# Half-row query stacks for two cross-attention groups, and one group's row sums taken earlier, in a two-attention transformer layer

## What is computed

```python
xn1 = _ln(x, g1, be1)
sa = _mha(xn1, xn1, Wq_s, bq_s, Wk_s, bk_s, Wv_s, bv_s, causal=True)
x = x + (sa @ W1 + b1)
xn2 = _ln(x, g2, be2)
ca = _mha(xn2, encoder_out, Wq_c, bq_c, Wk_c, bk_c, Wv_c, bv_c, causal=False)
x = x + (ca @ W2 + b2)
xn3 = _ln(x, g3, be3)
ff = jax.nn.relu(xn3 @ Wf1 + bf1) @ Wf2 + bf2
return x + ff
```

## Time and profile before

| | |
|---|---|
| median of three runs | 587.0 us |
| profiled execution, its time | 590.07 us |
| its span, first to last instruction | 588.2 us |
| mean granted clock of TensorE | 0.927 |
| PE busy | 490.6 us (83%) |
| DVE, ACT, POOL busy | 333.1, 316.0, 189.6 us |
| DMA moved | 48.11 MB, mean 82 GB/s |

### The profile page before, as it was taken

How to read it: one execution, slowest core, us unless ns; L and a number is a source line. 1 busy time by engine, 2 the same in 40 slices (tenths; PEclk the granted TensorE clock), 3 DMA queues, 4 the chain that set the end, 5 groups by cost and what they waited for, 6 DMA issues and landing times.

```text
span 588.2 us, 8820 instructions
## 1 busy us (share of the span) xinstructions
PE 490.6 (83%) x3296; PEld 284.2 (48%) x3296; DVE 333.1 (57%) x645; ACT 316.0 (54%) x622; POOL 189.6 (32%) x291
## 2 busy tenths in 40 slices
PE   1588974999999999989988888685379897999887
PEld 1375651443434343444433234341235176888877
DVE  3155885878788787867864044253455275363340
ACT  3674420757676767645576767355043972445360
POOL 2498870131212121221213424215611193030200
PEclk9989998899999999989999999788558788999999
DMA  8145846016162525250112774215941520101001
GB/s 284 58 134 177 203 139 119 0 26 105 35 109 60 94 45 106 56 90 2 34 34 79 162 148 79 57 33 156 176 95 23 145 60 0 37 1 37 19 18 37
DMA packets 31082, 48.11 MB, mean 82 GB/s; under 512 B 8832, under 2 KB 25728, under 8 KB 28928
## 3 DMA queue, kind: packets, MB, share of 16 engines
q1 hardware_dynamic: 30972, 47.54, 35.1%
q10 hardware_dynamic: 68, 0.02, 0.0%
HBM read 30.66 MB, written 12.03 MB: 73 GB/s over the span
## 4 chain that ended last, share of the span: by engine, by line
PE 59%; DVE 13%; ACT 9%; DMA 9%; issue 3%; POOL 2%; SPq 2%; ACTq 0%; DVEq 0%
PE ps L1197 12%; PE ps L1058 11%; PE ps L1167 9%; PE ps L1114 9%; PE ps L1278 6%; DVE max_a L1355 5%; PE ps L1136 4%; ACT arena_p L926 4%; DMA stacks<-shift_t 3%; PE ps L1044 3%; DMA stacks<-qc_parts 2%; PE ps L1153 2%; DVE hid_r L1458 2%; PE ps L1118 2%; DVE max_b L1355 2%
## 5 line engine op out<-in xcount | busy, mean ns | idle before, releaser
L926 ACT ACTIVATE arena_p<-ps 128x512 f32<-128x512 f32 (+4 forms) x416 | 191.4, 543 | 150.8 <-PE ps L1167 149.8
L1355 DVE TENSOR_REDUCE max_a<-ps 128x1 f32<-128x512 f32 (+4 forms) x280 | 158.9, 619 | 73.9 <-PE ps L1114 61.8
L1114 PE MATMUL ps<-stacks 96*128 96x77 bf16 (+4 forms) x640 | 139.0, 293 | 31.1 <-DMA stacks<-qc_parts 18.2
L1167 PE MATMUL ps<-stacks 99*128 99x512 bf16 (+1 forms) x448 | 142.6, 352 | 16.6 <-ACT arena_p L926 7.7
L1114 PEld LDWEIGHTS ps<-stacks 96*128 96x128 bf16 x640 | 55.5, 106 | 97.1 <-DVE max_a L1355 38.2
L1197 PE MATMUL ps<-arena_p,v_group 128*32 128x512 f32 (+3 forms) x896 | 95.9, 541 | 0.3 <-POOL arena_p L790 0.3
L790 POOL TENSOR_SCALAR_AFFINE_SELECT arena_p<-arena_p 128x512 f32<-128x512 f32 x64 | 39.9, 635 | 161.4 <-ACT arena_p L926 161.4
L1167 PEld LDWEIGHTS ps<-stacks 99*128 99x128 bf16 x448 | 42.3, 100 | 80.5 <-ACT arena_p L926 37.1
L1355 DVE TENSOR_REDUCE max_b<-ps 128x1 f32<-128x384 f32 (+3 forms) x88 | 52.9, 635 | 22.6 <-PE ps L1118 22.3
L1058 PE MATMUL ps<-wf2r,hid_r 128*128 128x256 f32 x384 | 47.2, 284 | 4.9 <-DVE hid_r L1458 3.8
L732 POOL TENSOR_TENSOR xs<-xs,row 128x256 f32<-128x256 f32 x48 | 39.6, 856 | 33.3 <-DVE xn L1312 33.3
(11 more groups left out here) (79 smaller groups left out, 501.3 us busy)
## 6 DMA issues: line engine op xcount, KB each, us to landing
arena_h<-out_t SPq DMA_DIRECT2D x16, 256.0 KB, 4.3
recips<-recip_rows SPq DMA_DIRECT2D x8, 512.0 KB
q_parts<-parts SPq DMA_DIRECT2D x8, 384.0 KB, 2.6
k_parts<-parts SPq DMA_DIRECT2D x8, 384.0 KB, 2.7
qc_parts<-parts SPq DMA_DIRECT2D x8, 384.0 KB, 3.0
stacks<-qc_parts SPq DMA_DIRECT2D x8, 384.0 KB, 6.4
stacks<-q_parts SPq DMA_DIRECT2D x7, 384.0 KB, 5.2
stacks<-k_parts SPq DMA_DIRECT2D x7, 384.0 KB, 7.6
```

The source lines that it names most:

```text
L926: nc.scalar.activation(probs[0:a.kp, a.probs_slot(g, ui), h, k * BANK:k * BANK + width], ps[0:a.kp, unit % S_BANKS, 0:width], ACT.Exp, sca ...
L1114: ins = nc.tensor.matmul(m_bank(use)[:, o:o + w], q_stack[0:ROWS, slot, h, t * P:(t + 1) * P], k_self[0:ROWS, slot, h, s0:s0 + w] if a.cau ...
L1167: ins = nc.tensor.matmul(ps[:, unit % S_BANKS, lo - k * BANK:hi - k * BANK], k_rows(a, ROWS_S, g, h, i * P), q_stack[:, a.slots[g % a.nb], ...
L1355: nc.vector.tensor_reduce(dst, m_bank(use)[:, 0:nh * w].rearrange("p (h w) -> p h w", h=nh), AX.X, ALU.max).then_inc(use_read, 1)
```

## The change

The query parts of groups 4 and 5 go to a DRAM tensor of their own, `qh_dram`, in which the 512 rows of a chunk lie together. Their stacks are loaded by halves: three DMAs of 192, 128 and 64 KB for chunk 2's rows, as soon as chunk 2's store for this pair has landed, and three more for chunk 3's. In the list the loads become: group 4 first half 27.5, group 5 first half 28.5, group 4 second half 31.5, group 5 second half 31.55, group 6 whole at 31.6 (was 40.0). The stack in SBUF is laid out half by half; chunks 4 to 7 of a group wait for its second half, chunks 0 to 3 for the first only.

For cross group 1 the copy of the second half of the product moves from 19.24 to 16.5, its packing from 20.15 to 16.6, its reciprocal, store and spread from 23.4 to 17.5, 17.6 and 17.7; its division stays behind chunk 3's last split. The packing of group 2 moves from 27.15 to 31.58, between the half loads and the load of group 6, and the packing of group 3 (33.75) now stands behind the load of group 6. The spread of group 3 moves from 56.0 to 53.4, ahead of the load of group 7.

```diff
+HALVED = (4, 5)
-            add(nxt + (0.46 + 0.5 * n) * CROSS_US, "copy", CROSS, g, n)
+            add(END + 16.5 if (g, n) == (1, 1) else nxt + (0.46 + 0.5 * n) * CROSS_US, "copy", CROSS, g, n)
         if g < NG - 2:
-            add(nxt + 1.1 * CROSS_US, "packed", CROSS, g)
-        if g == 1:
-            add(nxt + 1.6 * CROSS_US, "inverted", CROSS, g)
-            add(nxt + 1.62 * CROSS_US, "stored", CROSS, g)
-            add(nxt + 1.64 * CROSS_US, "spread", CROSS, g)
-            add(nxt + 2.9 * CROSS_US, "divided", CROSS, g)
+            add(END + (16.6, 31.58)[g - 1] if g in (1, 2) else nxt + 1.1 * CROSS_US, "packed", CROSS, g)
+    add(END + 17.5, "inverted", CROSS, 1)
+    add(END + 17.6, "stored", CROSS, 1)
+    add(END + 17.7, "spread", CROSS, 1)
+    add(END + 31.9, "divided", CROSS, 1)
-    add(END + 56.0, "spread", CROSS, 3)
+    add(END + 53.4, "spread", CROSS, 3)
-    for g, t in zip(range(NG // B, NG), (31.5, 31.6, 40.0, 53.5)):
-        add(END + t, "load", CROSS, g)
+    for g, half, t in ((4, 0, 27.5), (5, 0, 28.5), (4, 1, 31.5), (5, 1, 31.55), (6, None, 31.6), (7, None, 53.5)):
+        add(END + t, "load", CROSS, g, half)
...
+    qh_dram = nc.dram_tensor("qc_half_parts", (PARTS, 2, 2, GW, CHUNK), BF16).ap()
+        q_cross = q_stack.rearrange("p n h t -> p n (h t)").rearrange("p n (s h t) -> p n s h t", s=2, h=GH)
+                if 4 * (n // 2) + 2 * hh == HALVED[0]:
+                    a = qh_dram[:, n % 2, :, :, :]
+                    return CHUNK, BQ_C + hh, [(a.rearrange("p g r t -> (g r) p t"), 0, CHUNK)]
...
+            def load_half_stack(g, half, arrived, blk, part, n, same):
+                rows_of = qh_dram[part:part + (1 if same else n), half, g - HALVED[0], :, :]
+                rows_of = rows_of.rearrange("p (d h) t -> d p (h t)", d=D)
+                to = q_cross[blk * D:(blk + n) * D, CROSS.slots[g % CROSS.nb], half, :, :].rearrange("p h t -> p (h t)")
+                sp.dma_start(to, rows_of.to_broadcast([D, n, GH * CHUNK]) if same else rows_of).then_inc(arrived, 16)
...
+                        g, half = what
+                        for n in range(2) if half is None else [half]:
+                            u = U_QC + 2 * (2 * (g // (NG // B)) + n) + g % (NG // B) // 2
+                            sp.wait_ge(parts_out[u % 4], parts_landed(u))
+                        load_stacks(a, g, range(len(Q_RUNS)), half)
...
+                    if not a.causal and g in HALVED:
+                        pe.wait_ge(q_half[g % 2], 16 * len(Q_RUNS))
+                    else:
+                        pe.wait_ge(s.q_in[g % a.nb], 16 * n_loads)
+                elif not a.causal and g in HALVED and t == CT:
+                    pe.wait_ge(s.q_in[g % a.nb], 16 * len(Q_RUNS) * (g // a.nb + 1))
```

More of the change, by code:

```diff
@@ L259, in order @@
     for g, t in enumerate([7.1 * SELF_US, 7.15 * SELF_US, 7.2 * SELF_US, END + 0.5]):
-        add(t, "load", CROSS, g)
-    for g, t in zip(range(NG // B, NG), (31.5, 31.6, 40.0, 53.5)):
-        add(END + t, "load", CROSS, g)
+        add(t, "load", CROSS, g, None)
+    for g, half, t in ((4, 0, 27.5), (5, 0, 28.5), (4, 1, 31.5), (5, 1, 31.55), (6, None, 31.6), (7, None, 53.5)):
+        add(END + t, "load", CROSS, g, half)
     w2 = END + 70.0
@@ L430, in build @@
         half_in = sem("half_in")
+        q_half = [sem(f"q_half{p}") for p in range(2)]
         parts_out = [sem(f"parts_out{s}") for s in range(4)]
@@ L570, in load_run, with load_stacks @@
                              rows_of.to_broadcast([D, n, GH * T]) if same else rows_of).then_inc(arrived, 16)
-            def load_stacks(a, g, runs=range(2 * len(Q_RUNS))):
+            def load_half_stack(g, half, arrived, blk, part, n, same):
[3 more added lines that the diff above has]
+                sp.dma_start(to, rows_of.to_broadcast([D, n, GH * CHUNK]) if same else rows_of).then_inc(arrived, 16)
+            def load_stacks(a, g, runs=range(2 * len(Q_RUNS)), half=None):
                 s, slot = of[a], a.slots[g % a.nb]
@@ L583, in load_stacks @@
                 for n in runs:
-                    if n < len(Q_RUNS):
+                    if half is not None:
+                        load_half_stack(g, half, s.q_in[g % a.nb] if half else q_half[g % 2], *Q_RUNS[n], True)
+                    elif n < len(Q_RUNS):
                         load_run(q_dram if a.causal else qc_dram, q_stack[0:ROWS, slot, :, :], g, s.q_in[g % a.nb],
@@ L772, in split_shift @@
                 pool.wait_ge(maxima, n + 1)
-                m = max_a[:, g % 2, :, :].rearrange("p h i -> p (h i)")
+                m, to = max_a[:, g % 2, :, :].rearrange("p h i -> p (h i)"), neg_m[:, :]
+                if not a.causal and g in HALVED:
+                    m = max_a[:, g % 2, :, :].rearrange("p h (s i) -> p s h i", s=2)
+                    to = to.rearrange("p (s h i) -> p s h i", s=2, h=GH)
                 base = 5 * n
-                pool.tensor_scalar(neg_m[:, :], m, -1.0, None, ALU.mult).then_inc(shift_step, 1)
+                pool.tensor_scalar(to, m, -1.0, None, ALU.mult).then_inc(shift_step, 1)
                 pool.wait_ge(shift_step, base + 1)
@@ L1095, in k_rows, with q_columns @@
                 return k_self[0:n, a.slots[g % a.nb], h, lo:lo + P] if a.causal else k_ctx_row[0:n, at:at + P]
+            def q_columns(a, g, n, h, lo, hi):
+                slot = a.slots[g % a.nb]
+                if a.causal or g not in HALVED:
+                    return q_stack[0:n, slot, h, lo:hi]
+                t0 = lo // CHUNK * CHUNK
+                return q_cross[0:n, slot, lo // CHUNK, h, lo - t0:hi - t0]
             def chunk(use, a, g, c):
@@ L1106, in chunk @@
                         n_loads += 2 * (len(QP) - len(Q_RUNS))
-                    pe.wait_ge(s.q_in[g % a.nb], 16 * n_loads)
+                    if not a.causal and g in HALVED:
+                        pe.wait_ge(q_half[g % 2], 16 * len(Q_RUNS))
+                    else:
+                        pe.wait_ge(s.q_in[g % a.nb], 16 * n_loads)
                     if g == 0 and not a.causal:
                         pe.wait_ge(s.k_in, 16 * len(KP))
+                elif not a.causal and g in HALVED and t == CT:
+                    pe.wait_ge(s.q_in[g % a.nb], 16 * len(Q_RUNS) * (g // a.nb + 1))
                 diagonal = a.causal and s0 + w == (t + 1) * P
@@ L1113, in chunk @@
                     o = (h - h0) * w
-                    ins = nc.tensor.matmul(m_bank(use)[:, o:o + w], q_stack[0:ROWS, slot, h, t * P:(t + 1) * P],
+                    ins = nc.tensor.matmul(m_bank(use)[:, o:o + w], q_columns(a, g, ROWS, h, t * P, (t + 1) * P),
                                            k_self[0:ROWS, slot, h, s0:s0 + w] if a.causal
@@ L1168, in score @@
                                                k_rows(a, ROWS_S, g, h, i * P),
-                                               q_stack[:, a.slots[g % a.nb], h, q0 + lo - off:q0 + hi - off],
+                                               q_columns(a, g, ROWS_S, h, q0 + lo - off,
+                                                         q0 + hi - off),
                                                start=True, stop=True)
```

## The result

The changed kernel takes 592.08 us (median of ten runs, 590.13 to 593.85); the kernel before, in ten runs on the same chip, 587.06 (585.53 to 590.26). The ratio is 1.0071, 95% interval 1.0053 to 1.009. It is slower by 0.71%, or 4.2 us of 587 (the two medians alone lie 5.0 us apart, inside the interval's 3.1 to 5.3), and so outside the 2.9 us that I had called no change.

A forecast was written before the change was run, and what follows sets the result against it. The DMA queue and SP's order were taken to bound 405 to 439 us. Score 0 of group 5 coming 2.3 us later, halved by the clock to +1.15 with group 1's 0.46 inside, gave +1.2: 588.2 us, range 584.4 to 591.8.

The forecast's parts named there:

- within 0.5%: Whole kernel: time within about 2.9 us of the kernel before, either way; chance 0.60.
- rival 2: Halves at 2.25 us or above, SP late, group 3's sums at 426.0, group 7's load put off 4.0: +4, 591.0; chance 0.22.
- The bound: From 405 to 439 us the DMA queue and SP's filling order limit the kernel, no engine's arithmetic.
- Group 1, +0.46: Group 1's reciprocal ahead of chunk 2's norm on DVE delays the block up to the stores by 0.46 us, bounds 0 and 0.55.
- The halves: Groups 4 to 6: data 4 us earlier, but group 3's sums at 424.4 keep group 4's shift issue at 425.9, as before.
- The spread: Group 3's spread ahead of group 7's load puts that load off 3.0 us, to 438.35; score 0 of group 5 +2.3.
- The clock: Clock back no later than before, at 445.4; leftover 2.3 us of PE work then runs at twice the speed: +1.15.
- To the end: Behind 445 us the order is the old one and everything shifts alike.
- The signs: Profile after: group 3's reciprocal at 424 to 425, PE waiting 3 to 4 us for group 7, landing near 438.
- the slower side: Whole kernel: slower by more than 2.9 us; chance 0.23.
- Rival 1: Faster: group 3's sums at 423.2, group 7's load put off only 2.0, clock maybe sooner: -1 to -3.5, 585.0; chance 0.20.
- Rival 3: From 405 to 439 us the halves gain nothing in the full queue; only the reciprocal's 0.46 is left: 587.5; chance 0.08.

The follow-up runs named there:

- after_spread_back: The changed kernel with group 3's spread put back behind group 7's load: 588.0 us, ratio 1.0002 to the kernel before.
- halves_pack3_first: The changed kernel with group 3's spread back behind group 7's load and group 3's packing ahead of group 6's load: 584.11 us, ratio 0.9954 to before.
- best: The changed kernel with group 3's packing ahead of group 6's load, its spread last, all spreads on 16 engines, group 1 at its old place: 578.3 us, ratio 0.9843.
- pack3_group1_back: halves_pack3_first with group 1's copy, packing, reciprocal, store and spread at their old places: 584.07 us, ratio 0.9933 to the kernel before.

## Why the prediction was right or wrong

The direction was that of the forecast. By the ratio, 1.0071 times 587.0, the time is 591.2, inside the stated 584.4 to 591.8; the median itself, 592.08, lies 0.3 us above the upper end. The forecast was +1.2 us and the change costs 4.2, and within 0.5%, which I thought likeliest, was missed. That the range held at all is partly luck: it reached that far for rival 2, whose late sums and late SP did not happen; only its last term did.

- **The bound.** Right: the stretch from 405 to 439 is set by the DMA queue's order, and all the runs that moved the time moved only entries of that queue or gave one of its transfers more rows. That no engine's arithmetic limits it holds before; once group 4 comes early, POOL's split of the weights is in the way until 15.0 us after the last division.
- **Group 1, +0.46.** Right in kind: PE's idle time ahead of the turn rose by 0.37 us (1.82 to 2.19). In the time it can't be told.
- **The halves.** Group 3's reciprocal was put at 424.4, which is 18.5 us after the last division as the prediction had that; it came at 18.9. Group 4's shift was to be issued where it was: 20.3 us after the division, 20.5 before. These terms held to 0.4 us. That the gain at group 4 would be caught by the sums was right as well; that this was the whole gain was not seen until the packing was moved: 2.7 us below before.
- **The spread, the step that failed.** I had bounds of 2.0 and 4.0 for how far it puts off group 7's load, and took 3.0, by its bytes. Issue to use went from 7.5 to 11.6 us: 4.2, the upper bound and a little more. The term was even smaller than it looks: I added the 3.0 to the old landing at 435.35 and not to the later issue at 428.5, so that from issue to landing I allowed 9.85 us, 2.4 more than before. The row of 0.47 for 4.0 us was the right row and I read it rightly, as half of the engines; I then priced the spread by its bytes, as if the other half could take up the slack. The runs speak for the busy half: with the same bytes on 16 engines the load was used 8.7 us after its issue, and in the changed kernel the wait ends with 2.5 us at a share of 0.36. That the load's own pieces on a busy engine wait for all of the spread's is inferred from these numbers. The load also went out 0.6 us later after the last division than before (23.0 against 22.4), where I had 0.2. Score 0 of group 5 came 37.5 us after the division in place of 33.7: +3.8, where my times gave +1.8 beside group 1's 0.46.
- **The clock.** Halving what is left over was right: +3.8 us at score 0 of group 5 became +1.9 at the output rows (42.0 against 40.1). The stretch from 439.2 to 445.4 ran at 0.64, where it had 0.50: the clock was back at about 443.7, 39.4 us after the last division, and before at about 445.3, 39.9 after it. So it came back no later, as I had said.
- **To the end.** The profile has +1.7 us from the last division to the end and +0.34 between the first division and that one. The runs say 4.2. The other 2 us or so no trace shows: there is one profile of each kernel only, and behind the output rows the two take the same time (142.6 and 142.4 us).
- **The signs.** Group 7 landed by the clock of the trace near 438 (438.89), which looks like the forecast's place; but this execution reached the last division 1.7 us sooner than the forecast had it, so it is a match by luck, and counted from that division it is 2.2 us late (34.6 in place of 32.4). The wait for it was 6.08 us and not 3 to 4.
- **Rival 2** needed sums at 426.0 and a late SP. Neither happened; its put-off of 4.0 did. It had the right time for a reason that is right in one term of three, and 0.23 was too little for the slower side. **Rival 1** needed the load put off by 2.0 only and didn't happen. **Rival 3**, the halves gain nothing, is what after_spread_back measured (1.0002), again by another way: a wait that was put behind the load, not a full queue.

## What to carry to other kernels

In a stretch ruled by one DMA queue, list for each transfer who waits for it and when, and put small ones that hold an in-order engine (sums for a reciprocal, a shift) ahead of the large loads; here a load whose first half arrives 8 us sooner was worth nothing until one packing moved, and 2.7 us after. Look also at what else runs on the engines where the work would now fall, here a split of weights on POOL that had been out of the way. When a transfer uses only some of the DMA engines, price what stands behind it by its time on those engines, not by its bytes, and see whether its source can be given more rows. An early reciprocal or spread with no early reader only moves work ahead of somebody who waits.

## What the runs showed of the hardware

A broadcast of 0.52 MB from 8 rows ran at a DMA share of 0.48 (127 GB/s, about 4.1 us for all of it); from 16 rows at 0.89 (236 GB/s, about 2.2 us), for one more store of 32 KB, with which SP's next issue came 1.9 us after the reciprocal in place of 1.4. A full-width load queued behind it was used 11.6 us after its issue in the one case and 8.7 and 9.5 in the other. A DVE operation on 128x16 values took 3.27, 3.11 and 1.30 us in the changed kernel, halves_pack3_first and best, in place of 0.17 to 0.18, and ended each time 0.03 us after a POOL operation of 4.50 us on 128x2048 values that was running; why, no run asks. And the granted clock differs between executions that wait alike: 0.83 and 0.50 from 429 to 439.2 us in halves_pack3_first and pack3_group1_back, after nearly the same work and waits (1.92 and 0.22 us, 1.97 and 0.22 us). What decides when it comes back was not tried; single profiles a us apart should be read with that in mind.
